# Second matrix phase of a graph layer with Strassen's seven products on pairs of row tiles, narrow columns computed apart, on one core

## The reference, cut to what matters

```
edge_index = stack([src, dst])                    # 5000 edges among 10000 nodes, 1024 features
x = x + gnn(layernorm(x), edge_index, W, b)       # h = x W^T + b; weighted sums of neighbours' rows
x = x + ffn(layernorm(x), ...)
# ffn: base_out   = x base_W^T + base_b           (1024 -> 1024)
#      shared_out = (x shared_A^T) shared_B^T     (rank 16)
#      logits = x router_W^T + router_b           (6 experts), softmax, two largest kept
#      routed_out = sum over experts of weight * (x routed_A^T) routed_B^T   (rank 16 each)
```

## Time and profile before

| | us |
|---|---|
| median of three runs | 2139.61 (2138.91 to 2141.74) |
| profiled execution, device time | 2142.19 |
| its span, first to last instruction | 2140.2 |
| TensorE busy in the span | 2051.7 (96%) |
| VectorE, ScalarE, GpSimd busy | 1321.2, 704.2, 856.1 |

### The profile page before, as it was taken

How to read it: one execution, slowest core, us unless ns; L and a number is a source line. 1 busy time by engine, 2 the same in 40 slices (tenths; PEclk the granted TensorE clock), 3 DMA queues, 4 the chain that set the end, 5 groups by cost and what they waited for, 6 DMA issues and landing times.

```text
span 2140.2 us, 34026 instructions
## 1 busy us (share of the span) xinstructions
PE 2051.7 (96%) x11145; PEld 1885.8 (88%) x11145; DVE 1321.2 (62%) x3853; ACT 704.2 (33%) x1236; POOL 856.1 (40%) x934
## 2 busy tenths in 40 slices
PE   7999999999999999739999999999999999999999
PEld 6777777777777788539999999999999999999999
DVE  6877878787776666625555555554555555455553
ACT  4455555555555555401112111121211112121111
POOL 1802333333325200165554454544445454445520
PEclk9999999999999999969999999999999999999999
DMA  6523434343444434633333333333333333333311
GB/s 247 200 104 141 167 133 174 132 172 134 170 127 152 144 140 156 220 81 84 95 87 89 95 80 95 81 95 90 84 96 76 96 84 90 93 82 95 78 50 40
DMA packets 126936, 248.63 MB, mean 116 GB/s; under 512 B 53005, under 2 KB 55901, under 8 KB 126806
## 3 DMA queue, kind: packets, MB, share of 16 engines
q1 hardware_dynamic: 77462, 226.31, 30.1%
q0 software_dynamic: 49344, 20.85, 7.8%
HBM read 266.46 MB, written 125.55 MB: 183 GB/s over the span
## 4 chain that ended last, share of the span: by engine, by line
PE 55%; POOL 1%; DMA 1%; issue 0%; DVE 0%; POOLq 0%
PE bo L1106 15%; PE bo L1107 15%; PE bo L1108 15%; PE bt L1138 3%; PE bo L1297 2%; PE bo L1301 2%; PE bo L1299 2%; DMA acc<-h_rows,row_now 1%; POOL acc L685 1%; PE bt L1291 0%; DVE st L1689 0%; POOL pw L759 0%; DVE acc L1714 0%; POOL tick_pool L551 0%; POOLq L685 0%
## 5 line engine op out<-in xcount | busy, mean ns | idle before, releaser
L1106 PE MATMUL bo<-base_hi,z_hi 128*128 128x380 f32 (+1 forms) x1896 | 653.3, 345 | 1.5 <-ACT z_hi L1086 1.5
L1107 PE MATMUL bo<-base_lo,z_hi 128*128 128x380 f32 (+1 forms) x1896 | 639.8, 337 | 0.0
L1108 PE MATMUL bo<-base_hi,z_lo 128*128 128x380 f32 (+1 forms) x1896 | 639.3, 337 | 0.0
L685 POOL DMA_INDIRECT acc<-h_rows,row_now x312 | 494.3, 1584 | 125.0 <-issue 124.9
L1127 PE MATMUL bo<-wr_hi,left_hi 128*128 128x512 f32 x1008 | 403.8, 401 | 6.6 <-ACT bo L951 3.8
L1131 PE MATMUL bo<-wr_hi,left_lo 128*128 128x512 f32 x1008 | 395.1, 392 | 0.0
L1129 PE MATMUL bo<-wr_lo,left_hi 128*128 128x512 f32 x1008 | 394.9, 392 | 0.0
L1106 PEld LDWEIGHTS bo<-base_hi,z_hi 128*128 128x128 f32 x1896 | 358.3, 189 | 1.8 <-ACT z_hi L1086 1.8
L1108 PEld LDWEIGHTS bo<-base_hi,z_lo 128*128 128x128 f32 x1896 | 359.3, 189 | 0.0
L1107 PEld LDWEIGHTS bo<-base_lo,z_hi 128*128 128x128 f32 x1896 | 358.8, 189 | 0.0
L576 POOL TENSOR_TENSOR xpw<-xpin,neg_half 128x1 f32<-128x1 f32 x79 | 72.5, 917 | 551.5 <-DVE xpin L1322 551.5
(11 more groups left out here) (174 smaller groups left out, 2839.0 us busy)
## 6 DMA issues: line engine op xcount, KB each, us to landing
xn<-x SPq DMA_DIRECT2D x79, 512.0 KB, 4.1
r_rows<-xn SPq DMA_DIRECT2D x79, 512.0 KB, 2.7
acc<-r_rows SPq DMA_DIRECT2D x79, 512.0 KB, 4.5
out<-acc SPq DMA_DIRECT2D x79, 512.0 KB, 3.4
h_rows<-hrow SPq DMA_DIRECT2D x144, 256.0 KB, 2.4
acc<-h_rows,row_now POOLq DMA_INDIRECT x312, 4.2
base_raw<-base_t SPq DMA_DIRECT2D x8, 571.0 KB, 6.8
wr_raw<-w_t SPq DMA_DIRECT2D x16, 256.0 KB, 6.6
```

The costliest lines, as they stand in the source:

```text
L685: nc.gpsimd.indirect_dma_start(to[:], None, h_dram, bass.IndirectOffsetOnAxis(ap=row_now[q][:, r:r + 1], axis=0), bounds_check=NPAD - 1, o ...
L1106: nc.tensor.matmul(ps, hi[:, k, :], m_hi[:, k, n], start=(k == 0), stop=False)
L1107: nc.tensor.matmul(ps, hi[:, k, :], m_lo[:, k, n], start=False, stop=False)
L1108: return nc.tensor.matmul(ps, lo[:, k, :], m_hi[:, k, n], start=False, stop=(ends and k == KB - 1))
```

## The change

The second phase now works on the first tile singly (plain products of halves) and then on 39 pairs of tiles with Strassen's seven products for the 1024 wide columns. One turn of the loop is four pairs.
- PE, for a pair: seven products of 12 matmuls with 512 columns (`product2`); four times three matmuls of 512 columns for the low-rank part (`low`); the 118 narrow columns apart, with the weights stationary and the two tiles' 256 rows moving (`narrow`, 24 matmuls), whose result is copied by ACT, transposed to rows (two transposes) and, after routing of both tiles at once, transposed back (two); 16 transposes of the normalised tiles.
- ACT and DVE, for a pair: high and low parts of eight left blocks instead of four halves of tiles; four sums of blocks on DVE (`sums2`), three copies of transposed blocks and one copy between PSUM banks on ACT; the output leaves PSUM in six steps (`weighed_sum` x4, `added_bank` x2) instead of six of `finish`. Routing is done once for both tiles. Normalising a tile is two half-width ACT instructions instead of one.
- POOL issues the same gathers, two of the same round for a pair behind one wait. SP loads three pairs ahead.
- The four differences of wide weights are made beside the first phase: in 16 of its pair steps SP loads four 128x128 pieces, POOL makes four results (`differences`), and SP stores them (`store_piece`) into a DRAM tensor. At the end of the first phase seven 1 MB blocks of weights are loaded into buffers as they come free (`load_right`, `SLOT_OF`), and split there; three of them (T2, T3, T4) are split behind the start of the second phase.
- A semaphore counts two DMAs of a round where each gather had one of its own.

The core of the diff (the per-engine steps; lines that are removed stand above in the kernel):

```
+    def tile(self, a, t):
+        return 2 * (self.i + a) + 1 + t
+    def acc(self, a, t):
+        return (2 * (self.q + a) + 1 + t) % (2 * DEEP)
...
+            def load_right(n):
+                if n in (T1, T2, T3, T4):
+                    of = t_dram[(T1, T2, T3, T4).index(n)]
+                else:
+                    v, h = {B11: (0, 0), B21: (1, 0), B22: (1, 1)}[n]
+                    of = base_t[half(v), HCOLS + h * HALF:HCOLS + (h + 1) * HALF]
+                sp.dma_start(wr_raw[SLOT_OF[n]][:], of.rearrange("(k p) n -> p k n", p=P)) \
+                    .then_inc(weights_in[n], 16)
...
+            def load_piece(i):
+                k, c = i // 4, i % 4
+                if i > 0:
+                    sp.wait_ge(piece_out, 64 * i)
+                for n in range(4):
+                    a, z = n // 2 * HALF + k * P, HCOLS + n % 2 * HALF + c * P
+                    sp.dma_start(piece[:, n, :], base_t[a:a + P, z:z + P]).then_inc(piece_in, 16)
...
+            def differences(i):
+                pool.wait_ge(piece_in, 64 * (i + 1))
+                for to, a, c, after in ((3, 3, 1, 0), (1, 1, 0, 1), (0, 3, 0, 2), (2, 2, 0, 3)):
+                    if after:
+                        pool.wait_ge(piece_ok, 4 * i + after)
+                    nc.gpsimd.tensor_tensor(piece[:, to, :], piece[:, a, :], piece[:, c, :],
+                                            ALU.add if to == 0 else ALU.subtract) \
+                        .then_inc(piece_ok, 1)
             for p in range(PAIRS):
                 if p + 1 < PAIRS:
                     rstd(first(p + 1) + 1)
...
+            def add_pair(s, a, r):
+                for t in range(2):
+                    n = t * ROUNDS + r
+                    add_rows(acc[s.acc(a, t)], row_now[s.mod(a, 2)][:, n:n + 1],
+                             g_in[s.mod(a, 2)])
+            def added(s, a, r):
+                pool.wait_ge(g_in[s.mod(a, 2)], 32 * (ROUNDS * s.uses(a, 2) - ROUNDS + 1 + r))
...
             def step(s):
+                c = 22 + 4 * (s.q % 2)
                 if s.has(2):
+                    added(s, 2, 1)
+                    carry_wait(c)
+                    add_pair(s, 2, 2)
+                if s.has(1):
+                    power(s.tile(1, 1))
+                if s.has(2):
+                    added(s, 2, 2)
+                    carry_wait(c + 1)
+                    add_pair(s, 2, 3)
+                if s.has(3):
+                    added(s, 1, 3)
+                    slots_of(s, 3)
+                    rest_in(s, 3)
+                    carry_wait(c + 2)
+                    add_pair(s, 3, 0)
+                if s.has(2):
+                    power(s.tile(2, 0))
+                if s.has(3):
+                    added(s, 3, 0)
+                    carry_wait(c + 3)
+                    add_pair(s, 3, 1)
+            pipeline(pool, step, PAIRS2 - 2)
...
+            def norm(n, a, *waits):
+                act.wait_ge(acc_scales_ok, n + 1)
+                for wait in waits:
+                    act.wait_ge(*wait)
+                for v in range(2):
+                    ins = nc.scalar.activation(z_half[v][:], acc[a][:, half(v)], ACT.Identity,
+                                               bias=shift[:], scale=scale[:])
+                ins.then_inc(z_ok, 1)
+            def y_high(p, n, raw, *waits):
+                for wait in waits:
+                    act.wait_ge(*wait)
+                nc.scalar.activation(y_hi[n].rearrange("p k n -> p (k n)"), raw, ACT.Copy) \
+                    .then_inc(y_hi_ok, 1)
...
             def step(s):
+                p = s.pair(0)
+                narrow_out(p, 2)
                 if s.has(1):
+                    norm(s.tile(1, 0), s.acc(1, 0), (narrow_done, p + 2))
+                y_high(p, S4, ys4[:], (y_sum_ok, 4 * p + 4),
+                       *([(y_done, y_product_at(s.pair(-1), S4))] if s.has(-1) else []))
+                exponent(p, 2)
+                if s.has(1):
+                    first_row2(s.pair(1), ())
+                    first_row_right2(s.pair(1), y_product_at(p, A12))
+                    norm(s.tile(1, 1), s.acc(1, 1), (za_done, 2 * p + 6))
+                hidden_high(p, 2)
+                if s.has(1):
+                    second_row2(s.pair(1), ((y_done, y_product_at(p, A22)),))
+                    act.wait_ge(f_ok, f_at(p, F_C21))
+                    begin_second2(s.pair(1), s.mod(1, 2))
...
+            def narrow(nt):
+                ps = narrow_bank[0:HCOLS, 0:nt * P]
+                for k in range(KB):
+                    hi, lo = (row_hi, row_lo) if k < 4 else (right_hi, right_lo)
+                    m_hi, m_lo = hi[:, 0:nt, k % 4, :], lo[:, 0:nt, k % 4, :]
+                    nc.tensor.matmul(ps, narrow_hi[:, k, :], m_hi, start=(k == 0), stop=False,
+                                     skip_group_check=True)
+                    nc.tensor.matmul(ps, narrow_lo[:, k, :], m_hi, start=False, stop=False,
+                                     skip_group_check=True)
+                    last = nc.tensor.matmul(ps, narrow_hi[:, k, :], m_lo, start=False,
+                                            stop=(k == KB - 1), skip_group_check=True)
+                last.then_inc(narrow_done, 1)
...
+            def low(ps, t, v):
+                nc.tensor.matmul(ps, hs_hi[:, t, :], bl_hi[:, v, :], start=False, stop=False,
+                                 skip_group_check=True)
+                nc.tensor.matmul(ps, hs_hi[:, t, :], bl_lo[:, v, :], start=False, stop=False,
+                                 skip_group_check=True)
+                nc.tensor.matmul(ps, hs_lo[:, t, :], bl_hi[:, v, :], start=False, stop=True,
+                                 skip_group_check=True).then_inc(low_done, 1)
...
             def step(s):
+                p, q = s.pair(0), s.mod(0, 2)
+                ready(p, S1)
+                if s.has(-2):
+                    pe.wait_ge(f_ok, f_at(s.pair(-2), F_C12))
+                elif s.has(-1):
+                    pe.wait_ge(f_ok, 2)
+                product2(third_bank[q][:], S1, T1, True)
+                narrow_to_rows(p, 2)
+                ready(p, S2)
+                pe.wait_ge(y_begun, p + 2)
+                if not s.has(-1):
+                    split(T2)
+                product2(second_bank[:], S2, T2, False)
                 if s.has(1):
+                    transpose_a(s.pair(1), ((y21_ok, p + 1), (y_lo_ok, y_at(p, A22))))
+                product2(first_bank[q][:], A12, B21, False)
+                hidden_to_columns(p, 2)
+                ready(p, S3)
+                pe.wait_ge(f_ok, f_at(p, F_C12A))
+                if not s.has(-1):
+                    split(T3)
+                product2(second_bank[:], S3, T3, False)
+                hidden_ready(p)
+                if not s.has(-1):
+                    split("step")
+                low(second_bank[:], 1, 1)
+                low(first_bank[q][:], 0, 0)
+                if s.has(1):
+                    ready(s.pair(1), A11)
                     if s.has(-1):
...
+            def pair_statistics(s, a, t):
+                dve.wait_ge(g_in[s.mod(a, 2)], 32 * ROUNDS * s.uses(a, 2))
+                acc_statistics(s.tile(a, t), s.acc(a, t))
...
+            def weighed_sum(a, t, v, bank, *waits):
+                for wait in waits:
+                    dve.wait_ge(*wait)
+                av = acc[a][:, half(v)]
+                nc.vector.scalar_tensor_tensor(av, av, dis[:, bass.ds(t, 1)], bank, ALU.mult,
+                                               ALU.add).then_inc(f_ok, 1)
+            def added_bank(s, t, v, bank, before_it, *waits):
+                dve.wait_ge(f_ok, f_at(s.pair(0), before_it))
+                for wait in waits:
+                    dve.wait_ge(*wait)
+                av = acc[s.acc(0, t)][:, half(v)]
+                nc.vector.tensor_tensor(av, av, bank, ALU.add).then_inc(f_ok, 1)
...
             def step(s):
+                p, q = s.pair(0), s.mod(0, 2)
                 if s.has(-1):
+                    b = Pair(s.k, s.q - 1)
+                    added_bank(b, 0, 1, third_bank[1 - q][:], F_C12A, (low_done, 4 * p + 2))
+                if not s.has(0):
+                    return
+                y_low(p, S4, ys4[:])
+                choose(p, 2)
+                weighed_sum(s.acc(0, 0), s.tile(0, 0), 1, second_bank[:],
+                            (y_done, y_product_at(p, S2)))
+                hidden(p, 2)
                 if s.has(1):
+                    pair_statistics(s, 1, 1)
+                    y_low(s.pair(1), A11, y11[:])
+                    acc_scales(s.tile(1, 1))
+                hidden_low(p, 2)
+                weighed_sum(s.acc(0, 1), s.tile(0, 1), 1, second_bank[:], (low_done, 4 * p + 3))
+                added_bank(s, 1, 1, third_bank[q][:], F_C22A, (y_done, y_product_at(p, S1)))
+                weighed_sum(s.acc(0, 0), s.tile(0, 0), 0, first_bank[q][:], (low_done, 4 * p + 4))
+                if s.has(1):
```

(88 more changed lines are left out.)

786 lines of the change are left out of this document (445 added, 341 removed).

## The result

2186.06 us, the median of four runs (2182.27 to 2201.22), against 2139.93 before: ratio 1.0228, 95% interval 1.0178 to 1.0278. The change makes this kernel slower, by 1.8 to 2.8%. 2120 us was forecast, with faster as the likelier sign; the time lies inside the range of 2070 to 2190. The profiled execution took 2182.27 us, its span is 2180.5. Three single executions further on (2206.99 us of e3, 2451.95 of e9, and 11608.33 of the kernel before, measured beside e12) came out far above the others of the same kernel and are in no ratio, though the medians count them.

What follows compares the result with a forecast made beforehand. It took a ring through POOL, 29.2 us a pair, as the bound over PE's 26.8: 987 + 38 x 29.2 + 20.0 + 4.1 = 2120.7, + 2.0 = 2122.7, less 2.6 for the median: 2120 us, range 2070 to 2190.

Steps and rivals of the forecast that it cites:

- The ring: Second-phase loop from POOL's powers through DVE, ACT, PE and back: 28.9 us a pair, 29.2 with an allowance for gathers.
- POOL's half: The ring's part from first power over two gathers and their landing to second power: 12.5 us; other half 16.4.
- PE's own sum: TensorE's work for a pair in the second phase: 26.8 us, 3.1 less than before.
- the ring is shorter: Rival: overlapping gather issue or cheaper normalisation halves put a pair between 26.8 and 28.4 us, 2029 to 2090; chance 0.15.
- In general 1010.5 + 38 T: Total time in us, T being the us of a pair; equals the old time at T = 29.7.
- First phase ... hidden, nothing: Added first-phase DMAs and POOL operations: no cost if hidden in POOL's waits; uncovered 1 to 2 us a step, 30 at most.
- Start of the second phase: First S1 product of pair 0 on PE starts near 987 us (975 to 1000), POOL's first carrier near 904.5.
- The tail: End of the second phase: last step 20.0 us, then 4.1 for eviction and store.
- The clock falls at each wait: Rival: half clock on PE after its 2.4 us wait in each step, T = 30.9, 2185 us; chance 0.27.
- Gathers land late: Rival: POOL's gathers land after 5.7 instead of 3.8 us, T = 31.1, 2192 us; chance 0.10.
- POOL's own round: All of POOL's gathers, landings, powers and slots for a pair: 26 us, fitting in with little room.
- Narrow columns gain nothing: Rival: PE's narrow columns cost 5.4 us instead of 2.9, T about 29.9, 2147 us; chance 0.04.

Runs made afterwards that it cites:

- e3: The changed kernel with the second phase written out for every pair instead of a loop of four pairs a turn: 2138.62 us, ratio 1.0000.
- e9: e6 with POOL's power for the next pair's second tile moved to the head of POOL's step: 2056.59 us, ratio 0.9596.
- e12: e3 with three short DVE operations left out of every choice of experts (equal gates not told apart): 2138.0 us, ratio 1.0004.
- e8: The kernel before the change with its second phase written out for every tile: 2141.16 us, ratio 1.0002.
- e2: The changed kernel with six matmuls of unused result put in front of PE's wait before the low-rank products: 2162.19 us, ratio 1.0107.
- e5: e1 with the second phase written out for every pair, as in e3: 2094.35 us, ratio 0.9794.
- e6: e5 with POOL's differences moved as in e4, and pair 0's A11 low part made earlier on DVE: 2082.9 us, ratio 0.9725.
- e1: The changed kernel with hidden_high and hidden_low moved in front of the next pair's second tile's normalisation and scale: 2087.09 us, ratio 0.9768.
- e4: The changed kernel with POOL's differences moved from behind the counts to right behind its second power: 2185.0 us, ratio 1.0209.
- e7: e3 with the fourth round of gathers left out for every pair: 2138.4 us, ratio 0.9984.
- e10: The changed kernel with only POOL's power for the second tile moved to the head of its step: 2183.67 us, ratio 1.0214.

## Why the forecast was wrong

**The ring exists, and its sum was right within half a microsecond.** Its halves were read from one step of e3 on POOL's timeline, first power to second power to first:

```profile
1146.12 0.95 POOL L894 TENSOR_TENSOR pw<-pin,neg_half 128x1 f32<-128x1 f32 x1 [7.33 <-DVE pin L2029]
...
1157.13 1.11 POOL L894 TENSOR_TENSOR pw<-pin,neg_half 128x1 f32<-128x1 f32 x1
...
1174.93 0.94 POOL L894 TENSOR_TENSOR pw<-pin,neg_half 128x1 f32<-128x1 f32 x1 [6.22 <-DVE pin L2029]
```

POOL's half 12.1 us (1146.12 to 1158.24; forecast 12.5), the other 16.7 (forecast 16.4), together 28.8 against 28.9. Together they are the length of that step whichever chain sets it, so they show how the time splits and not that the ring holds. What holds is seen at DVE's scale. In 19 of e3's 38 steps DVE waits under 0.5 us for the second power, which comes right behind `pin`, and all of these but one take 28.6 to 28.8 us: the second chain below. In the other 19 POOL is later (waits of 0.54 to 2.2 us) and the step is longer, up to 31.9: the ring. Alone, in e12, the ring takes 28.2 to 28.6 in its shorter steps. With the pairs written out the mean is 29.11, forecast 29.2; that they agree so closely is in part luck, since 0.2 us of the 29.11 is half clock (five steps of 38, 1.6 us each), which the forecast's T leaves out. PE's wait in the ordinary step is 1.13 us and not 2.4. PE's own sum was 26.8; without waits a step takes 27.25, since a product's first matmuls step at 0.3 instead of 0.23. The narrow columns cost 0.12 us each, as the 262-column row had said. What I missed beside the ring is a second chain: the narrow rows, `choose`, `hidden`, the second tile's statistics, power, scale, normalisation, `hs_hi`, `hs_lo`. It gives the same 28.6 us, so it cost nothing here, but it would have made the rival "the ring is shorter" worthless.

**The step that failed is "In general 1010.5 + 38 T".** It took T, a sum of links priced from straight code, as the time of every step, and left the loop out. Written out, the changed kernel takes 2138.62 us; looped, 2186.06. These 47 us are the turns (DVE stands 3.8 to 4.1 us, seven times), 0.4 to 0.7 us a step in the two chains, and the half clock that the longer waits bring: 17 slow steps instead of 5. The kernel before has the same loop and pays nothing (e8, 1.0002), because its PE never waits. Its DVE has no stand over 0.6 us without a releaser in the second phase, so nothing in its trace shows the price, but the code showed the loop, and the forecast had just put every engine but PE on the path.

**"First phase ... hidden, nothing" failed.** POOL has 158 us of slack, but it was DVE that had none: 0.4 us on its residual updates is passed on to PE, and so is the 0.13 by which the low part just before them is longer (0.81 us beside POOL, 0.68 apart). By the transposes 9.2 us are lost in 16 steps (7.6 net at its end). The bound of 1 to 2 us a step was for POOL; the step measures 0.65. In the forecast I had weighed the Trainium skill's rule on the shared port (SBUF — State Buffer, "SBUF: two separate sides": a VectorE instruction with two SBUF inputs and a GpSimd one that reads SBUF exclude each other) for the power and the gathers, and not for these operations. The traces agree in that both lose: 3.81 and 2.88 us together, 2.07 and 2.47 apart.

**Start of the second phase**: 987 forecast, 1002.5 measured. 10.9 us are the later first phase: POOL's first carrier is at 915.43 instead of 904.5. The rest is order: PE waits 8.08 us for A11's low part, which stands on DVE behind the splits of T3 and T4.

```profile
984.13 0.77 PE L1488 MATMUL bo<-wr_hi,row_hi 128*128 128x512 f32 x1 [8.08 <-DVE row_lo L2114]
```

With the differences moved S1 starts at 997.4, with that low part moved as well at 990.1 and 995.0. The tail was as forecast.

**The sum of the errors**: 2120 + 15.5 (start) + 38 x (30.36 - 29.2) = 44 gives 2179.6. The forecast had taken off 2.6 us from the profiled execution to the median; with them it is 2182.2, and the profiled execution took 2182.27 (this time the median lies 3.8 us above it). In the same way e3, without the loop, is 2120 + 16.6 - 3.4 + 2.6 = 2135.8, against 2135.92 in its profiled execution: all but the loop would have made no change of the time, where 20 us less were forecast.

**The rivals.** "The clock falls at each wait" gave 2185 us, which is the time measured, but for another reason in part. Its mechanism is real: e2 gives back 24 us by filling the wait, and 17 of 38 steps are struck, above the third at which it decides. It does not make up the difference by itself; most of the longer waits it needs come from the loop, and that its time fits so well is luck. "Gathers land late" did not decide here (landings of 3.6 us in the middle of eight gathers, 4.3 beside a store), but a late landing ahead of the second power bounded e5 and e6 at 28 us. POOL's own round, forecast 26 us, has 3 us of room in e9's 27.25. "Narrow columns gain nothing" was wrong.

## What to carry to other kernels

A loop's turn and its register-dependent waits are free only while the engine that bounds the stage has a backlog; when a change puts a chain of short steps on the path, price the loop too, or write the stage out and measure. Before pricing a wait, look at what is queued in front of it for no reason: here one small rounding stood behind a normalisation, and moving it forward was worth 99 us, more than twice what the change had lost. When a wait is removed expect the next one (here a power behind GpSimd's landings) to show within a few steps, and look for a second chain of equal length before blaming the first.

## What the runs showed of the hardware

- How PE's clock answered a wait, over the 234 steps that have exactly one in eight of these traces (the change, e1 to e4, e7, e10, e12): none of 141 waits under 1.6 us was followed by matmuls at 0.43 us, 3 of 12 from 1.6 to 1.79, 36 of 65 from 1.8 to 2.09, 14 of 16 above. Waits of the same length, 1.82 to 1.85 us, had both outcomes; a slow stretch costs the step 1.6 us.
- DVE stood 2.4 to 2.7 and 1.4 to 1.6 us with no releaser at each of the seven turns of the changed kernel's loop, and each stand had an 8 KB block of instructions on a DMA queue 1.7 to 2.2 us before its end. In the written-out kernels (e3, e9) no stand of DVE over 0.6 us without a releaser appears in the second phase, though instruction blocks are loaded there too (77 in the second phase of e3).
- A POOL operation on four 128x128 blocks and a DVE update with two SBUF operands that run together take 1.74 and 0.41 us longer than apart.
- Six more matmuls in a step made the kernel 24 us faster.
